# A ring of four places and a lag of four units for the second expert product, with the high halves rounded behind the gates

## The reference

```
xn = _layernorm(x)
q, k, v = split_heads(xn @ Wq + bq), split_heads(xn @ Wk + bk), split_heads(xn @ Wv + bv)
attn = softmax(where(causal, q @ k.T / sqrt(dk), -inf)) @ v
topk_w, topk_idx = top_k(softmax(xn @ gate_w.T), 4)      # weights are then divided by their sum
a = silu(xn @ w_gate[e]) * (xn @ w_up[e]) * combine[:, e]   # for each expert e
y = sum over e of a @ w_down[e]
y = y + silu(xn @ sw_gate) * (xn @ sw_up) @ sw_down
out = x + (attn @ Wo + bo) + y
```

## Time and profile before

| | |
|---|---|
| median of 3 runs | 1243.69 us (1237.26 to 1247.66) |
| the profiled execution | 1237.0 us, of which the span is 1235.4 us |
| PE busy in the span | 953.5 us (77%) |
| DVE busy | 852.5 us (69%) |
| ACT busy | 629.5 us (51%) |
| POOL busy | 598.5 us (48%) |
| mean granted clock of PE, as a share of full speed | 0.903 |

### The profile page before, as it was taken

The page is one execution under the profiler, slowest core; times in us unless marked ns, Lnnn a source line. Parts: engine busy times, 40 slices in busy tenths (PEclk is TensorE's granted clock), DMA queues, the critical chain, the costliest instruction groups (busy, mean ns, idle before and its releaser), DMA issues.

```text
span 1235.4 us, 25494 instructions
## 1 busy us (share of the span) xinstructions
PE 953.5 (77%) x8010; PEld 466.1 (38%) x8010; DVE 852.5 (69%) x1992; ACT 629.5 (51%) x1219; POOL 598.5 (48%) x571
## 2 busy tenths in 40 slices
PE   1877436868789786989888979886888896988475
PEld 1444312433334333444343444443334443443233
DVE  5888796758768576677776776775676766687243
ACT  3777402434436464456565744564656543665231
POOL 6544347777621564246565642564646424553000
PEclk9888757989989798999998999898989899999788
DMA  5999753344362656266666653665555626476512
GB/s 163 286 304 288 235 184 92 86 98 100 98 149 71 115 89 121 45 129 98 122 108 112 107 112 68 115 107 102 98 119 94 117 45 122 77 126 101 108 38 34
DMA packets 186587, 147.70 MB, mean 120 GB/s; under 512 B 111618, under 2 KB 170259, under 8 KB 185939
## 3 DMA queue, kind: packets, MB, share of 16 engines
q0 software_dynamic: 42208, 61.67, 29.0%
q1 hardware_dynamic: 144258, 84.46, 26.3%
HBM read 72.52 MB, written 57.80 MB: 105 GB/s over the span
## 4 chain that ended last, share of the span: by engine, by line
PE 39%; DVE 17%; DMA 12%; SPq 8%; issue 7%; ACT 4%; POOL 0%; ACTq 0%; DVEq 0%
PE outs L1259 8%; PE gup L1245 8%; DVE part L1321 8%; PE pvp L1169 7%; DMA HT<-logits 5%; PE smp L1125 4%; PE outs L1176 4%; PE stp L1150 3%; DMA HT<-hx 3%; SPq L139 2%; DVE th L1373 2%; SPq L1010 2%; DVE hf L1378 2%; DMA rsum_d<-recs 2%; PE turn L1215 1%
## 5 line engine op out<-in xcount | busy, mean ns | idle before, releaser
L1491 ACT ACTIVATE probs<-stp 128x1024 f32<-128x1024 f32 (+1 forms) x320 | 300.5, 939 | 345.2 <-PE stp L1150 336.1
L1321 DVE TENSOR_REDUCE part<-smp 128x2 f32<-128x256 f32 (+2 forms) x372 | 346.1, 951 | 128.5 <-PE smp L1125 69.7
L1259 PE MATMUL outs<-dn_w,HT 128*128 (+5 forms) x1040 | 186.2, 290 | 100.6 <-DMA HT<-logits 53.9
L1245 PE MATMUL gup<-gu_w,XC 128*128 (+1 forms) x1152 | 219.2, 329 | 14.9 <-DVE hf L1378 14.5
L1259 PEld LDWEIGHTS outs<-dn_w,HT 128*128 128x128 f16 (+2 forms) x1040 | 91.4, 99 | 262.9 <-issue 185.9
L959 POOL DMA_INDIRECT XG<-xrow_d,slots x144 | 146.8, 1020 | 89.7 <-DMA out<-Y 43.6
L966 POOL DMA_INDIRECT acc_d<-Y,slots x72 | 115.4, 1603 | 154.3 <-ACT Y L1525 145.8
L966 POOL DMA_INDIRECT out<-Y,slots x72 | 116.5, 1618 | 146.4 <-ACT Y L1525 129.8
L1125 PE MATMUL smp<-Ks,Qs 48*128 48x128 f16 (+2 forms) x744 | 127.4, 349 | 59.4 <-DVE part L1321 49.3
L1169 PE MATMUL pvp<-probs,Vs 128*32 128x512 f32 (+3 forms) x1536 | 171.3, 519 | 0.9 <-DVE probs L1421 0.7
L1150 PE MATMUL stp<-Qs,Ks 50*128 50x512 f16 (+3 forms) x768 | 135.5, 340 | 18.0 <-DMA Qs<-nm 13.0
(11 more groups left out here) (177 smaller groups left out, 1114.8 us busy)
## 6 DMA issues: line engine op xcount, KB each, us to landing
rb<-rsum_d SPq DMA_DIRECT2D x60, 128.0 KB
Ks<-k_d SPq DMA_DIRECT2D x96, 64.0 KB
Qs<-q_d SPq DMA_DIRECT2D x96, 64.0 KB
v_d<-V SPq DMA_DIRECT2D x8, 544.0 KB, 4.9
Vs<-v_d SPq DMA_DIRECT2D x16, 272.0 KB, 3.4
acc_d<-YA SPq DMA_DIRECT2D x1, 4224.0 KB, 16.5
X<-L_attn_x POOLq DMA_DIRECT2D x8, 512.0 KB, 5.3
xrow_d<-XR SPq DMA_DIRECT2D x8, 512.0 KB, 5.2
```

Of the source, the lines that this page charges most:

```text
L1245: last = pe.matmul(gup[:, 0:2 * I], columns[:, a, h], weights_of(s.gu_w, P, e, b, h, slice(0, 2 * I)), start=n == 0, stop=n == 5)
L1259: last = pe.matmul(yp, HT[0:rows, v % TB, c], weights_of(s.dn_w, rows, e, b, slice(0, D)), start=begin and n == 0, stop=end and n == 4)
L1321: last = dve.tensor_reduce(part[:, g % 2, k0 // CH, :, j, t], banks[:, :, col:col + w], AX.X, ALU.max)
L1491: act.activation(to, of, ACT.Exp, scale=float(DK) ** -0.5 / QS ** 2).then_inc(exp_done, 1)
```

## The change

HT gets a fourth place (TB 3 to 4), and LAG goes from 3 to 4, so that the second half of unit v stands after the first half of v + 4 in the planner's list. On ACT `high_part` goes to the end of its slot, behind `gates` or `second_half`. To have room, `sel` is no tile of its own any more: it lies in the memory of `entry`, and is made after the scatter of the entries is done.

```diff
-        FB, XB, TB = 2, 3, 3
+        FB, XB, TB = 2, 3, 4
...
-        sel = sb("sel", [P, P])
+        sel = s.entry[:, :, :].rearrange("p i a -> p (i a)").bitcast(F32)[:, 0:P]
...
-        LAG, SPARE = 3, 4
+        LAG, SPARE = 4, 4
...
-            pool.memset(sel[:, :], 0.0).then_inc(a_const, 1)
             for x in HX:
                 pool.memset(x[:, P:2 * P], 0.0).then_inc(hx_clear, 1)
-            pool.wait_ge(a_const, 3)
-            pool.affine_select(out=sel[:, :], in_=sel[:, :], compare_op=ALU.not_equal, fill=1.0, base=-DK,
-                               pattern=[[-32, 4], [0, 32]], channel_multiplier=1).then_inc(sel_made, 1)
+            pool.wait_ge(a_const, 2)
...
+            pool.memset(sel, 0.0).then_inc(a_const, 1)
+            pool.wait_ge(a_const, 3)
+            pool.affine_select(out=sel, in_=sel, compare_op=ALU.not_equal, fill=1.0, base=-DK,
+                               pattern=[[-32, 4], [0, 32]], channel_multiplier=1).then_inc(sel_made, 1)
             for r in range(GB):
                 gather(r)
...
                     exps(g, n)
-                    if (g, n) in HIGH:
-                        high_part(HIGH[g, n])
                     if a is not None:
                         if SU <= a + 1 < SU + UT:
                             columns(a + 1 - SU)
                         gates(a)
                     elif z is not None:
                         second_half(z)
+                    if (g, n) in HIGH:
+                        high_part(HIGH[g, n])
```

More of the change, by code:

```diff
@@ L1196, in spread_sums @@
                     pe.wait_ge(ya_done, TT - KT // 2)
-                pe.matmul(smp[:, q, :], sel[:, :], rb[:, q], start=True, stop=True).then_inc(spread, 1)
+                pe.matmul(smp[:, q, :], sel, rb[:, q], start=True, stop=True).then_inc(spread, 1)
             def weights_of(t, rows, e, *ix):
```

## The result

| | before | after |
|---|---|---|
| median, beside each other on one chip | 1244.38 us (1237.26 to 1247.66) | 1183.99 us (1180.22 to 1193.99) |
| ratio | | 0.9535, 95% interval 0.9457 to 0.9612 |
| the profiled execution | 1237.0 us | 1193.99 us |
| PE busy in the span | 953.5 us (77%) | 947.3 us (79%) |
| DVE, ACT, POOL busy | 852.5, 629.5, 598.5 us | 854.0, 631.5, 598.0 us |

The change makes the kernel 4.65% faster. The profiled execution of before is at the lower end of its runs, that of after at the upper end, so the two traces differ by 43 us where the medians differ by 60. Two runs lay far above the others of their kernel (1712.68 us, one of ten with the ring alone, and 1186.6 us, one of four with the late addition); the ratios leave them out.

The account below looks back on a forecast made before the run. No engine is full; PE's waits for transpositions issued late from SP's queue at group borders set the time. Terms sum to 57 us, the check gave 43; 50 off 1237.0 us, plus 0.54%, gives 1193 us, range 1160 to 1226.

Parts of the forecast that it names:

- the sum of terms: Whole kernel: lag 59, clock 14, tanh 8.6, less 10.4 for late high parts and 14 for reciprocals, gives 57 us.
- The lag: PE's waits for HT at group borders: second halves one slot later end 59 of 91.5 us; 12 stay, 20 are last stretch.
- Done alike for all: Group 10's working applied to all borders: groups 3, 4, 6, 7, 10, 11, 12, 14 lose their waits but some 0.4 us.
- The last stretch, no gain: Near the end, behind POOL's addition of acc_d: PE's 17.03 us wait for HT ends as much later as it starts.
- The clock: PE's products behind seven ended waits run at a higher granted clock: 2.0 us each, 14 us gained.
- What is late next: Reciprocals over SP, needed by DVE at slot 6: waits at eight more borders, 1.8 us each, 14 us lost.
- The rival that made this chain the bound: Reciprocals late at slot 6 in all 14 borders, 2.5 us each: only 23 us gained, median 1221 us; chance 0.15.
- High part behind the gates: On ACT, 131 high parts leave the tanh's way: half of PE's 17.3 us wait for hf, 8.6 us gained.
- High part behind the second half: On ACT, 61 high parts now wait for PE's second product and Y, delaying DVE: 10.4 us lost.
- The slower rival: DVE held by high parts in 61 slots: 129 us lost against 73 gained, so 1300 us; chance 0.06.
- The check against groups 5, 9 and 13: Groups nearly without waits take 60.3 us, eleven others 64.2; if all ran like the three, 43 us go.

Follow-up runs that it names:

- the ring alone: Kernel before with four places in HT, LAG left at 3 and the high part at its old place: 1227.83 us, ratio 0.9949.
- the late addition: POOL's 4 MB addition of acc_d to out asked for only when the last Y is written: ratio 0.9451 on the kernel after, 0.987 on the kernel before.
- spread loads: SP's 12 loads of keys and queries issued one each in slots 5 to 16: 1159.65 us on the kernel after, 1207.61 us on the kernel before.
- the later reciprocals: Kernel after with DVE's multiplication by the reciprocals and the copy behind it moved from slot 6 to slot 7: 1160.71 us, ratio 0.9344.
- the third cure: DVE's reciprocal step moved to slot 7, added to the kernel after with loads one per slot and addition behind the last Y: 1103.1 us, ratio 0.8881.
- one cure on top of it: Kernel after with either loads one per slot (1159.65 us) or DVE's reciprocal step moved to slot 7 (1160.71 us).
- all three: Kernel after with loads one per slot, the addition behind the last Y and DVE's reciprocal step in slot 7: 1103.1 us, ratio 0.8881.
- two cures: Kernel after with loads one per slot in slots 5 to 16 and the addition asked for behind the last Y: 1142.03 us, ratio 0.9203.

## Why the prediction was right, and where it was not

The time (1193 forecast, 1183.99 measured) and its mechanism held. How near the number came is in part luck: the sum of terms gave 57 us, the check 43, and the middle, 50, was a compromise between them. The two traces differ by 43 us, the medians by 60 on one chip and by 47 on another, and the terms missed in both directions. The steps, one by one:

- **The lag** was sized a little too large: ahead of the last stretch 59 of 71 us were to end, and 48.6 did (71.2 to 22.7). The other 7 of the 55.5 us lie in the last stretch, where 5.53 of them came back as the wait for Qs. "Done alike for all" failed at the borders to groups 3 and 7, where a transposition is still behind sums and values and PE kept 3.52 and 3.07 us; group 8 kept 2.44 us where 1.6 was forecast, and group 1 6.7 where 5.6 was. The forecast's own 12 us also leave out the rests of some 0.4 us that it grants to eight groups.
- **The last stretch, no gain**: right in sum (150.0 to 151.5 us, and 17.03 against 11.40 + 5.53), wrong in its row: the wait did not stay one of 17 us for HT, because the maxima of group 15 were caught as well. The runs with the late addition show the cause.
- **The clock** was mis-sized: 14 us forecast, 3.2 measured in PE's work. (The figure scatters: 840.7 in a second execution of after, 828.9 with four places in HX at the same time.) The step took it that a border without a wait for HT is a border without a wait. But waits for Qs and for row maxima stand there too, and behind one of 1.43 us the clock was 0.57. In the runs with spread loads and with the later reciprocals PE's work fell by 17.6 and 16.1 us, and the third cure on top of two others took off 20.7.
- **What is late next** was the right chain and about the right size: 14 us forecast, and PE's waits for row maxima grew by 17.9 (10.0 in the second execution). But it was read at the wrong row: DVE's wait for rb was to grow to 24 us, and is 19.8 and 12.2 in the two executions. What counts is the row behind it, on PE. The rival that made this chain the bound had the mechanism, and so had the prediction's own term; moving the step one slot gave back more than the whole term, since it also took away waits that stood there before the change.
- **High part behind the gates**, 8.6 us by PE's waits for hf: that row did not move (17.3 to 17.8). The move alone gave 1.1% (0.4 to 1.9), and the change without it came out 0.5 to 1% slower, with intervals that overlap. Rows that moved are the waits for Y in the changed kernel (1.2 to 6.2 us without it) and for row maxima in the kernel before (45.4 to 40.0 us).
- **High part behind the second half**, -10.4 us: DVE's waits for it grew from 8.4 to 31.4 us, over twice the forecast, but for another reason. With four places in HX only 6.3 us stay, which bounds what a late Y does. The rest is ACT's wait for a place in HX, of which the prediction said that it would shrink (11.5 us); it grew to 38.6. The slip: ACT's high part asks for the transposition of three units back, one unit nearer than PE now does, so it is now the first to meet a late one. As the run with four places shows, this cost no time.
- **The slower rival** fell. The Trainium skill's rule behind it (TensorE: Matmul & The Clock Gate, section "Architectural detail: the array is 16× 32×32, not 1× 128×128") says that the queues of ScalarE and VectorE are strictly first in, first out. The trace agrees on the order, as in group 3, where the exponentials start only when the high part that stood 6.00 us has been taken up. But ACT is only 53% busy, and with four places in HX 25 of DVE's 31.4 us of waits went without any change of the time.
- **The check against groups 5, 9 and 13** was the best step, by the traces: it gave 43 us for the eleven other groups (0 to 13 without the three; the prediction writes 0 to 12), and groups 0 to 13 fell from 887.4 to 845.3 us, by 42.1 (45.3 in the second execution). Those eleven now take 60.6 us in the mean, against the 60.3 of the rate. Groups last 56 to 63 us, and 66 in group 1. A measured rate of slots without the fault holds the wait that takes its place, which the sum of terms had to guess: the rows of over 3 us for row maxima stood in groups 9 and 13 before the change. It is no floor, though: with the later reciprocals groups 5, 9 and 13 take 54.0, 56.3 and 54.9 us. And the reason given for the three, that they follow a group with projections, does not single them out: groups 6 and 10 do too, and waited 5.2 and 7.1 us.

Open is which rows pay for the high part's 1%, and how much of the lag's gain is PE's asking later and how much the transposition's earlier place on SP.

## What to carry to other kernels

A wait that is removed must be followed to the next one on the same engine: here part of PE's wait for a transfer became a wait for DVE a few slots later, and a small move of that step was worth about half as much as the change itself. Waits that come from bursts on a queue that only issues transfers (SP) can be met in two ways that add up here: a longer lag with the ring that it needs (3.6%), and spreading the bursts (2.4% alone, 6.5% with the change). A longer ring without the lag gave 0.5%, and a longer one in HX nothing. Stretches of the same kernel that lack the fault are a check on the sum of the waits; here, by the traces, they were nearer than the sum.

## What the runs showed of the hardware that was not expected

- Ending PE's waits could pay twice. For the same 7109 pieces PE's work took 843.7 us before the change, 822.9 and 824.4 us with one cure on top of it, and 803.4 us with all three, at mean granted clocks of 0.93, 0.95, 0.95 and 0.98 over the loop. From two cures to three, work fell by as much as idle time (20.7 and 19.8 us); from the kernel before to all three, by less than half as much (40.3 and 90.4); and with the change alone hardly (3.2 and 37.4).
- A stand of 1.43 us was followed by 3.96 us at a granted clock of 0.57, between the two levels of 1.2 and 2.4 GHz (0.5 and 1.0); it was 1.00 before the stand, and 1.00 again after those 3.96 us.
- The 4 MB addition, four issues of 3.49 us in all on POOL, went with waits of PE for transpositions of SP's queue of 17.0 us before and 11.4 after, and there with one of 5.53 us for the maxima; asked for later, it left none over 2.0 us in the last two groups in either kernel.
